# Mamba-2 mixer between two mixture-of-experts layers: decay exponents repeated by DMA instead of by TensorE

## The reference, cut to what matters

```python
def mixer(u):                                # u: layernormed, (2, 1024, 512)
    z, xBC, dt = split(u @ W_in.T)           # widths 1024, 1280, 16
    x, B, C = split(silu(causal_conv4(xBC))) # 1024 = 16 heads of 64; B, C: 128 each
    dt = softplus(dt + dt_bias); A = -exp(A_log)
    for t in range(1024):                    # per head h
        state = exp(dt[t] * A) * state + x[t] * (dt[t] * B[t])
        y[t] = C[t] @ state
    y = (y + x * D) * silu(z)
    y = y * rsqrt(mean(y * y) + eps) * norm_w
    return y @ W_out.T
```

## Time and profile before

| | us |
|---|---|
| median of 3 runs | 1654.26 |
| lowest and highest | 1643.24, 1655.32 |
| the profiled execution, its own time | 1652.43 |
| its span in the profile | 1650.7 |
| PE busy | 1554.2 |
| DVE, ACT, POOL busy | 1039.5, 751.8, 794.7 |
| mixer, first unit to last projection | about 536 to 1125 |

### The profile page before, as it was taken

The page is one execution under the profiler, slowest core; times in us unless marked ns, Lnnn a source line. Parts: engine busy times, 40 slices in busy tenths (PEclk is TensorE's granted clock), DMA queues, the critical chain, the costliest instruction groups (busy, mean ns, idle before and its releaser), DMA issues. The chain is left out here.

```text
span 1650.7 us, 24820 instructions
## 1 busy us (share of the span) xinstructions
PE 1554.2 (94%) x9018; PEld 1325.3 (80%) x9018; DVE 1039.5 (63%) x1712; ACT 751.8 (46%) x1290; POOL 794.7 (48%) x475
## 2 busy tenths in 40 slices
PE   6989999999999989989888999998989999999999
PEld 5767999999877778787767788777768999999877
DVE  6674566666476956767556766764664566666365
ACT  4312666666423544554255345434212666666411
POOL 2111777766444346435523553552111777766442
PEclk9999999999999999999899999997989999999999
DMA  7032677777352110120012002014032677677343
GB/s 285 26 105 65 243 262 272 249 269 273 101 187 82 64 52 1 39 77 1 1 52 65 1 15 75 2 36 147 26 105 71 235 264 269 253 263 267 113 154 127
DMA packets 70876, 214.49 MB, mean 130 GB/s; under 512 B 8096, under 2 KB 8096, under 8 KB 69856
## 3 DMA queue, kind: packets, MB, share of 16 engines
q1 hardware_dynamic: 48672, 155.18, 26.6%
q0 software_dynamic: 11360, 37.23, 7.7%
q10 hardware_dynamic: 10720, 20.45, 3.4%
HBM read 179.80 MB, written 33.03 MB: 129 GB/s over the span
## 5 line engine op out<-in xcount | busy, mean ns | idle before, releaser
L618 POOL TENSOR_TENSOR g_lo<-g_raw,g_hi 128x1408 fp32r<-128x1408 f32 x54 | 179.5, 3324 | 259.9 <-ACT g_hi L745 259.6
L618 POOL TENSOR_TENSOR u_lo<-u_raw,u_hi 128x1408 fp32r<-128x1408 f32 x54 | 174.3, 3227 | 68.9 <-ACT u_hi L745 68.9
L1642 PE MATMUL bank<-u_hi,xgT 128*128 128x352 f32 x624 | 169.6, 333 | 0.0
L1642 PE MATMUL bank<-g_hi,xgT 128*128 128x352 f32 x624 | 162.8, 323 | 0.0
L1665 PE MATMUL bank<-d_hi,hT 128*128 128x512 f32 (+1 forms) x468 | 160.2, 396 | 2.2 <-DVE hT L1046 1.8
L683 POOL TENSOR_TENSOR w_hl<-w_raw,w_hl 128x1024 fp32r<-128x1024 f32 x36 | 88.1, 2447 | 150.7 <-ACT w_hl L745 150.7
L1594 PE MATMUL bank<-xs,g_hi 128*128 128x512 f32 (+1 forms) x384 | 129.0, 418 | 5.6 <-DVE gate L1192 4.6
L793 ACT ACTIVATE gate<-bank 128x512 f32<-128x512 f32 (+1 forms) x48 | 28.6, 596 | 218.5 <-PE bank L1594 210.8
L1610 PE MATMUL bank<-d_hi,hT 128*128 128x512 f32 (+1 forms) x384 | 123.5, 394 | 4.8 <-DVE hT L1046 2.4
L1201 DVE TENSOR_TENSOR d_lo<-d_raw,d_hi 128x1024 fp32r<-128x1024 f32 x54 | 110.0, 2037 | 26.7 <-ACT d_hi L745 20.0
L1046 DVE TENSOR_TENSOR hT<-bank,hT 128x384 fp32r<-128x384 f32 x78 | 43.1, 552 | 129.2 <-ACT hT L745 129.2
(11 more groups left out here) (246 smaller groups left out, 3721.8 us busy)
## 6 DMA issues: line engine op xcount, KB each, us to landing
g_raw<-in_w_gate SPq DMA_DIRECT2D x54, 704.0 KB, 5.0
u_raw<-in_w_up SPq DMA_DIRECT2D x54, 704.0 KB, 6.9
d_raw<-in_w_down SPq DMA_DIRECT2D x54, 512.0 KB, 5.2
w_raw<-in_w_in SPq DMA_DIRECT2D x37, 512.0 KB
routed_y<-ys ACTq DMA_DIRECT2D x32, 512.0 KB
d_raw<-in_w_down SPq DMA_DIRECT2D x54, 192.0 KB, 5.7
token_x<-xn SPq DMA_DIRECT2D x8, 1024.0 KB, 4.8
X<-in_x SPq DMA_DIRECT2D x4, 1024.0 KB, 10.8
```

The lines of the kernel that those rows point to most:

```text
L618: pool.tensor_tensor(half_of(piece, 1, s), raw_at[piece][s % RING][:], half_of(piece, 0, s).bitcast(F), ALU.subtract)\
L1642: ins = pe.matmul(dst[:, 0:FE], xgT[:, n % 2, hx, kc], half_of(piece, hw, NS + j)[:, kc], start=(m == 0), stop=(m == 3 * KD - 1))
```

## The change: rows of running sums through DRAM

PE forms, beside cs and the totals, the sums once more transposed: a row for each tile and head of the block, 64 rows of 128 (`decays(j)`, now three matmuls and no more). This stands at the head of unit 7 (`CS_UNIT`), no longer behind unit 8. ACT copies the rows to `csT`, SP writes them to the DRAM tensor `cs_rows`, waits for that, and reads them back as four DMAs per tile, each repeating 4 rows of 512 bytes on all 128 partitions, straight into `L`. Those of tile n wait until PE has used that group of `L` for tile n−1; `m_E` therefore counts groups now.

ACT turns the raw cs[t] in `L` into relu(cs[s] − cs[t]), with cs[s] as the bias `cs_k`, one instruction for each head, waits for these four, and takes exp(−·) of the four heads in one instruction of 512 columns. The clamp keeps the elements with s > t at 1 or below, and DVE makes them zero by masking C·B once per tile: `GB[:, 0:P]` is bank 3 times `tri`, one 128x128 DVE instruction. ACT copies only B. The exponential of softplus moves from behind unit 6 to the head of unit 5, ahead of the first silu of z. The mask tile and its matmuls are gone; nothing changes in the expert layers but the mask tile's set-up.

```diff
--- before.py
+++ after.py
...
@@ -541,16 +545,33 @@
                     sp.dma_start(w_raw[:, j], w_in[j]).then_inc(m_raw[j], 16)
                 sp.dma_start(wdt_raw[:], w_dt).then_inc(m_wdt, 16)
 
-                with sp.Fori(0, BPB * NWU - 1) as i:
-                    for q in range(2):
-                        w = i * 2 + 2 + q
-                        sp.wait_ge(m_wlo, w - 1)
-                        u = sp.snap(w % NWU)
-                        sp.dma_start(w_raw[:, q], w_in[bass.ds(u, 1), :, :, :].rearrange("o p c n -> p (o c) n"))\
-                            .then_inc(m_raw[q], 16)
-
-                sp.wait_ge(m_wlo, BATCH * BPB * NWU - 1)
-                sp.dma_start(w_raw[:, 0], w_in[0]).then_inc(m_raw[0], 16)
+                def unit(w):
+
+                    sp.wait_ge(m_wlo, w - 1)
+                    sp.dma_start(w_raw[:, w % 2], w_in[w % NWU]).then_inc(m_raw[w % 2], 16)
+
+                def decay_rows(n):
+
+
+                    for g in range(HG):
+                        if n:
+                            sp.wait_ge(m_E, HG * (n - 1) + g + 1)
+                        first = n % TB * HEADS + g * GH
+                        row = cs_rows[first:first + GH, :].rearrange("(o r) n -> o (r n)", o=1)
+                        sp.dma_start(L[:, g * GH:(g + 1) * GH].rearrange("p h t -> p (h t)"),
+                                     row.broadcast_to([P, GH * P])).then_inc(m_Lraw[g], 16)
+
+                for b in range(NB):
+                    for u in range(NWU):
+                        if u == NWU - 1:
+                            sp.wait_ge(m_csT, b + 1)
+                            sp.dma_start(cs_rows, csT[0:NQ, :]).then_inc(m_rows, 16)
+                        w = b * NWU + u + 2
+                        if w <= NB * NWU:
+                            unit(w)
+                    sp.wait_ge(m_rows, (b + 1) * 16)
+                    for q in range(TB):
+                        decay_rows(b * TB + q)
 
             for k, what in enumerate(PLAN):
                 (ffn if what == "ffn" else mixer)(k)
@@ -968,18 +989,21 @@
                             else:
                                 if u == 5:
                                     conv_out(j * NCH + NCH - 1, NCH - 1)
+                                    after(m_dx, j + 1, BPB)
+                                    act.activation(d_e[:], d_z[:], ACT.Exp).then_inc(m_de, 1)
                                     act.wait_ge(m_wo_lo0, 2)
                                     act.wait_ge(m_wo_lo1, 2)
                                     after(m_yg, j * TB, TPB)
+                                if u == CS_UNIT:
+                                    after(m_cs, j + 1, BPB)
+                                    after(m_ncs, j + 1, BPB)
+                                    act.activation(csT[0:NQ, :], bank[2][0:NQ, 3 * NQ:3 * NQ + P], ACT.Copy).then_inc(m_csT, 1)
                                 for half in range(2):
                                     n = j * 8 + (u - 5) * 2 + half
                                     after(m_zp, n + 1, 8 * BPB)
                                     act.activation(zs[:, 2 * half:2 * half + 2, (u - 5) * WU:(u - 4) * WU],
                                                    bank[6 + half][:].rearrange("p (q n) -> p q n", q=2),
                                                    ACT.Silu).then_inc(m_z, 1)
-                                if u == 6:
-                                    after(m_dx, j + 1, BPB)
-                                    act.activation(d_e[:], d_z[:], ACT.Exp).then_inc(m_de, 1)
                         after(m_cs, j + 1, BPB)
                         after(m_ncs, j + 1, BPB)
                         cs, tot = bank[2][:, NQ:2 * NQ], bank[2][:, 2 * NQ:3 * NQ]
@@ -989,17 +1013,17 @@
                         for q in range(TB):
                             n = j * TB + q
                             for g in range(HG):
-                                after(m_B, HG * n + g + 1, HG * TPB)
-                                after(m_E, n, TPB)
+                                after(m_Lraw[g], n + 1, TPB, unit=16)
                                 for h in range(g * GH, (g + 1) * GH):
-                                    ins = act.activation(L[:, h], bank[g % 2][:, (h % GH) * P:(h % GH + 1) * P], ACT.Exp,
-                                                         bias=ncs[:, q * HEADS + h:q * HEADS + h + 1])
-                                ins.then_inc(m_L, 1)
+                                    ins = act.activation(L[:, h], L[:, h], ACT.Relu, scale=-1.0,
+                                                         bias=cs_k[:, q * HEADS + h:q * HEADS + h + 1])
+                                own.step(ins)
+                                group = L[:, g * GH:(g + 1) * GH]
+                                act.activation(group, group, ACT.Exp, scale=-1.0).then_inc(m_L, 1)
                                 if g == 0:
-                                    after(m_G, n + 1, TPB)
+                                    after(m_Gm, n + 1, TPB)
                                     after(m_D, n, TPB)
-                                    after(m_M, HG * n, HG * TPB)
-                                    act.activation(GB[:], bank[3][:, 0:2 * P], ACT.Copy).then_inc(m_Bt, 1)
+                                    act.activation(Bt, bank[3][:, P:2 * P], ACT.Copy).then_inc(m_Bt, 1)
                                 if g == 1 and q >= 1:
                                     y_hi(n - 1)
                             if q >= 1:
...
@@ -1421,8 +1447,8 @@
                                 softplus()
                         log1p()
                         after(m_cs, j + 1, BPB)
-                        own.step(dve.tensor_scalar(ncs[:], bank[2][:, NQ:2 * NQ], -1.0, None, ALU.mult))
-                        dve.tensor_tensor(d_p[:], bank[2][:, 2 * NQ:3 * NQ], ncs[:], ALU.add).then_inc(m_ncs, 1)
+                        own.step(dve.tensor_copy(cs_k[:], bank[2][:, NQ:2 * NQ]))
+                        dve.tensor_tensor(d_p[:], bank[2][:, 2 * NQ:3 * NQ], cs_k[:], ALU.subtract).then_inc(m_ncs, 1)
 
                         for q in range(TB):
                             n = j * TB + q
@@ -1435,12 +1461,14 @@
                             x_next = X[:, bass.ds(nxt, 1), :].rearrange("p o n -> p (o n)")
                             ln_stats([x_next], [q], l_var)
 
+                            after(m_G, n + 1, TPB)
+                            dve.tensor_tensor(GB[:, 0:P], bank[3][:, 0:P], tri[:], ALU.mult).then_inc(m_Gm, 1)
                             for half in range(2):
                                 hs = slice(half * DI // 2, (half + 1) * DI // 2)
                                 after(m_xt, 2 * n + half + 1, 2 * TPB)
                                 if half == 0:
                                     after(m_xw, n, TPB)
-                                    after(m_E, n, TPB)
+                                    after(m_E, HG * n, HG * TPB)
                                 ins = dve.tensor_tensor(heads_of(xdt[:, hs]), heads_of(bank[4 + half][:]),
                                                         each(dts[:, q * HEADS + half * HB:q * HEADS + (half + 1) * HB], HD),
                                                         ALU.mult)
...
@@ -1804,6 +1830,19 @@
                                     m += 1
                         ins.then_inc(m_out, 1)
 
+                    def decays(j):
+
+
+                        after(m_ap, j + 1, BPB)
+                        for dst, mat in ((1, tri_b), (2, ones_b)):
+                            for p in range(3):
+                                pe.matmul(bank[2][:, dst * NQ:(dst + 1) * NQ], mat[:], aparts[:, p],
+                                          start=(p == 0), stop=(p == 2))
+                        for p in range(3):
+                            ins = pe.matmul(bank[2][0:NQ, 3 * NQ:3 * NQ + P], aparts[:, p], tri_b[:],
+                                            start=(p == 0), stop=(p == 2))
+                        ins.then_inc(m_cs, 1)
+
                     for j in range(BPB):
                         pe.wait_ge(l_lo, i * TPB + (j + 1) * TB)
                         for u in range(NWU):
...
@@ -1862,36 +1902,9 @@
                                                 m += 1
                                     ins.then_inc(m_zp, 1)
 
-                        after(m_ap, j + 1, BPB)
-                        for dst, mat in ((1, tri_b), (2, ones_b)):
-                            for p in range(3):
-                                ins = pe.matmul(bank[2][:, dst * NQ:(dst + 1) * NQ], mat[:], aparts[:, p],
-                                                start=(p == 0), stop=(p == 2))
-                        ins.then_inc(m_cs, 1)
-
-                        def decays(n, q, g):
-
-                            if q == 0 and g < 2:
-                                after(m_pre, (j + 1) * NCH, BPB * NCH)
-                            else:
```

(18 more changed lines are left out.)

35 lines of the change are left out of this document (21 added, 14 removed).

## The result

| | before | changed |
|---|---|---|
| median, us | 1651.24 | 1701.75 |
| lowest and highest of 4 runs | 1643.24, 1655.32 | 1700.80, 1710.78 |
| span of the profiled execution | 1650.7 | 1699.0 |

The ratio is 1.0314, 95% interval 1.0277 to 1.0351: slower by 3.1%. Forecast were 1713 us, slower by over 1% with a chance of 0.87, and a range of 1674 to 1742.

The account below looks back on a forecast made before the run. The prediction took a closed chain per tile, not PE's work, as the bound: 12 × 2.96 us for later tiles plus 4 × 5.95 per block made 59.3 us, hence 1713 us, range 1674 to 1742.

Parts of the forecast that it names:

- The chain: Each tile: L times xdt, additions, product, features, y halves, projection, state; `decays` fills its waits, removal there worth nothing.
- The clock in the tiles: 12 later tiles: emptied waits drop PE to 1.2 GHz, 2.59 us in projection plus 0.37 before it, 2.96 us each.
- the one taken from the end of the turn: Slow-clock loss per later tile, copied from the turn's last projection, 8.32 us instead of 5.73: 2.96 us with its approach.
- ACT in the tile: Later tiles: ACT's longer groups cost nothing with the slow clock, about 0.45 us a tile without.
- The first tile: Each block's first tile: 0.7 us more before L times xdt, and 2.6 us more in it from slow clock.
- The exponential: Softplus's exponential and table loads lengthen the stall ahead of unit 6: 2.82 us, taken as 2.1 a block.
- The rows: DMA of rows into `L` lands in 2.0 us, before ACT is free, covered by its mask wait; cost 0.
- one of the three signs by which the prediction said it would be wrong: In the tiles, ACT's wait before its first group being for the rows; no size given.
- The signs: Expected trace: features at 4.0 us, PE idle 2.7, projections 8, tiles near 22, stall 6.2, first L times xdt 6.
- PE as the bound: Rival, whole kernel: all 56.6 us of removed PE work come back, about 1609 us; chance 0.06.
- The clock that stays up: Rival, tiles: C·B and features keep PE's clock up, 21.6 us more, 1676 us; chance 0.11.
- the third rival: Rows late by 1.3 us a tile or projections wholly at half clock, full silu stall: 92 us, 1746; chance 0.12.

Follow-up runs that it names:

- the filled kernel: The changed kernel with the 64 groups of `decays` matmuls put back on PE at their old places, results unread: 1685.85 us, ratio 1.0211.
- The filled first tiles: The changed kernel with five groups of unread matmuls on PE in each block's first tile only: 1696.26 us, ratio 1.0293.
- The kernel without the rows: The changed kernel without the DMA of rows into `L`; ACT takes relu of the triangle tile, decay values left out: 1707.31 us, ratio 1.0344.
- the thinned kernel: The kernel before with 8 of the 12 running-sum matmuls of each `decays` group left out, ACT's work unchanged: 1652.81 us, ratio 1.0022.

## Why the prediction was right

*The chain.* Right. The features start 3.97 us after L times xdt (3.98 in the earlier trace rows), released by POOL, and some 28 us less of matmuls in the kernel before gained nothing. That the work of `decays` in the waits was worth nothing is shown, not only argued, by that and by the filled kernel, which has all of it and is faster.

*The clock in the tiles.* The mechanism was right and the size too large: 2.96 us a tile forecast, 1.77 measured (21.2 over 12). The mis-sized term is the one taken from the end of the turn. Of it, the projection's loss was put at 2.59 us and was 1.6 (mean of the twelve 7.33 us), the way from features to projection at 0.37 and was 0.16. At the turn's end PE was idle for 3.80 us at a stretch and the features ran slowly (1.97 us); in the tile shown the wait was 2.55 behind C·B, the features still took 1.09 us, and the projection was slow only until about 652.0, 2.9 us of its 7.04. The text had said that the work of C·B speaks for a milder fall, and had given it no number. That C·B is the reason fits, but is not shown by itself: another tile with the same 2.55 us of idle time had its features at 1.97.

*ACT in the tile.* Put at nothing with the slow clock and at 0.45 us without. The features mostly ran at the full clock, so ACT was not free: it was 0.12 us late, and the projection 0.11. That is part of the 0.16 above, and about 1 us over the kernel.

*The first tile.* 0.7 us from the z units to L times xdt forecast, 0.65 measured. L times xdt itself was put at 2.6 us more with bounds of 0 and 3.7: it was 3.3, at the slow clock for its whole length. The filled first tiles showed it to be the clock. These 2.8 us more over the four blocks offset a little of what the tiles had too much.

*The exponential.* 2.65 us a block with the sums' matmuls forecast, 2.9 measured. The stall grew by 2.98. Behind the four stalls PE ran at 1.2 GHz for 16.5 us, before 20.9: at half the speed that gives back an estimated 0.55 us a block, where 0.7 had been taken. The trace shows each load at 1.28 us with the next instruction 0.02 us behind it, as before. The drain that the Trainium skill has behind a load (ScalarE: Activation LUTs, What ACT_TABLE_LOAD costs) is not seen.

*The rows.* Taken as 2.0 us to landing, they took 3.8, between the two figures of the earlier trace rows. Next to nothing came of it, but not for the reason given. The group was not there before ACT was free: ACT waited 5.29 us, and the wait was ended by the landing. That is one of the three signs by which the prediction said it would be wrong, and it came true. The cover was ACT's wait for the masked C·B, as the text says; it was just long enough, since C·B was ready when ACT's first group was done. That it sufficed is luck. And DVE's low half, and with it the projection, do wait for ACT. The kernel without the rows shows that earlier rows gain nothing, not that later ones would cost nothing.

*The signs.* Of the others, features at 3.97 us, idle time of 2.55 us and a stall of 6.40 fit 4.0, 2.7 and 6.2. L times xdt of first tiles took 7.1 and not 6, projections 7.33 in the mean and not 8, at 1.2 GHz for only part of their length, and most tiles 20.5 to 20.8 us and not 22.

*Rivals.* PE as the bound fell by the thinned kernel. The clock that stays up fell by the windows: it accounts for about 13 us in the first tiles and 12 × 1.6 = 19 in the later projections, 1.9% of the span. The Trainium skill's share of under 1% for the ramp in a typical kernel (TensorE: Matmul & The Clock Gate, Part 1: The HAM clock gate) does not hold for this one, where the clock falls again in each tile. In the third rival the sum was too small by its own terms: 1.3 us for the rows and 5.7 for a projection wholly at half clock make 7 us a tile, not 5, so 1770 and not 1746. It was far off either way.

What stays open is when exactly the clock falls and comes back. The z stretches show it best. Each holds one stall ahead of unit 6, of 3.34 to 3.42 us in the kernel before, and how long a stretch takes goes with how long PE ran at 1.2 GHz behind that stall. In the kernel before these were 3.4, 5.6, 5.7 and 6.2 us in stretches of 28.7, 29.6, 29.6 and 29.9; in its version with the shorter chain, which leaves the z units alone, one stretch had no slow time at all and took 27.1. That is how its z stretches came to be 3.8 us shorter in sum. The changed kernel has 3.4 to 3.6 us in three blocks (32.0 to 32.2) and 6.1 in the fourth (33.2). Why equal stalls are followed by such different times no experiment shows, nor why two tiles with the same waits differ.

## What to carry to other kernels

An engine that is busy for 94% need not be the bound: check whether each of its waits ends just when another engine's product arrives. If it does, the work between those waits is free, and taking it away gains nothing and can cost the clock. Shorten the chain first, then relieve the engine: here the relief alone, with its moved exponential, made the kernel 3.1% slower. The shorter chain alone made it 1.1% faster, most of it at the two turn ends, and both, with the exponential later and the first tiles filled, 1.5% faster.

## What the runs showed of the hardware

With idle stretches of 2.55 and 1.18 us before and after the features' 1.09 us, PE's granted clock went from 2.4 to 1.2 GHz in the tile shown; with 1.23 and 0.63 us, in the thinned kernel, the projection kept its 5.70 us. Matmuls of 64 columns with a weight load each took nearly twice as long at 1.2 GHz (7.08 against 3.68 us for 32 of them). Unread matmuls in such waits paid for themselves, 16 us in one case; in the first tiles alone they gave back 13 us in L times xdt, of which 3.5 were left in the span. ACT's table loads took 1.28 us each, with the next instruction 0.02 us behind. A read of 4 rows of 512 bytes repeated on 128 partitions, 256 KB in all, landed in 3.8 us in the median.
